# A decoder layer on one Trainium2 core: the five steps from sums to shares stand apart among the maxima

## The chip, the cores and the metric

The kernel runs on one core of one Trainium2 chip. The metric is the device time of one execution in microseconds (us). The engines are TensorE (PE in the rows; its weight loads are PEld), VectorE (DVE), ScalarE (ACT), GpSimd (POOL) and SyncE (SP), whose instruction stream issues most DMAs (SPq).

## The reference, cut to what matters

One decoder layer with normalisation ahead of each part, for x of 4 x 1024 x 256 in f32: self-attention (16 heads of 16, causal), cross-attention over 77 context rows with a mask, and a gated feed-forward part of width 768, each added to the residual. What the change touches is the softmax of both attentions:

```
scores = jnp.where(causal[None, None], scores, -jnp.inf)
attn = jax.nn.softmax(scores, axis=-1)
out = jnp.einsum('bhqk,bkhd->bqhd', attn, V).reshape(b, s, H * hd)
return out @ Wo.T + bo
...
attn = jax.nn.softmax(scores, axis=-1)
out = jnp.einsum('bhqk,bhkd->bhqd', attn, v)
```

## The kernel before, in words

The phases follow each other: projections, self-attention, a middle part (output projection, residual, normalisation, queries of the cross-attention), cross-attention, feed-forward. Every engine has its own program, and semaphores alone tie them together.

Both attentions work in 16 groups: GB = 4 groups for each of the 4 batches, HG = 4 heads and 1024 queries in each group. A batch is called b, a group g, and `b = g // GB - 1` in the code is the batch before the one that is being worked on.

Self-attention makes the scores twice. First TensorE makes them with queries on the partitions (`maxima`, lines 837 and 842), and VectorE takes the largest of each row (`item`, a reduction on line 767, one for each of 38 items of a group). The largest values are cut into two bf16 parts (`parts_of_max`, lines 777 to 782), turned by TensorE (line 832), copied to `mrow` (line 764) and sent by a DMA into two further rows of the queries (`stq`). Then TensorE makes the scores with keys on the partitions and the maximum taken away (`scores`, lines 856 and 860), ScalarE takes the exponential (line 814), and TensorE multiplies by the values (`products`, line 870), where a column of ones gives the sum of each softmax row. So in the loop of group g the maxima of group g + 1 stand among the scores and products of group g. Their order is a list, `ring`, of NMX = 40 items: 38 reductions and the two turned blocks `("t", 0)` (item 15) and `("t", 1)` (item 39). The order on TensorE is the list `plan`: nearly always one scores unit, one ring item, and now and then a pair of products of 16 matmuls each. The maxima use three banks of PSUM, so

```
need(t, s_mxe, N if N == N_AHEAD else N - 1 if N < N_AHEAD + 2 else N + 1 - NMB)
```

lets TensorE begin item N when VectorE is through with item N - 3 (NMB = 3). In `plan`, the first pair of products stands right behind item 6, the second right behind item 10, the third behind item 19, the fourth behind item 27, the fifth behind item 36.

The sums of a batch, 16 heads x 1024 queries, are gathered by DMA into `den` (128 x 128 f32); the last of them is the DMA on line 728 (self) or line 1508 (cross) of the function that stores a group's output. When the four groups of a batch are stored, `shares` (self) or `shares3` (cross) makes the shares 1/sum and cuts them into three bf16 parts: a reciprocal (lines 937, 1525), a copy to bf16 (940, 1528), a subtraction (943, 1531), a copy to bf16 (940, 1528) and a subtraction (945, 1533). Each step waits for the semaphore of the step before. Ahead of the first step VectorE waits for the stores of the four groups (`us`, `xus`). SyncE then writes the parts to DRAM (`store_shares`, `store_shares3`, which wait for all five steps) and reads them back; they are used a group or more later.

In self-attention `shares` stands on VectorE in the loop of groups 5, 9 and 13, behind all 39 items of the next group. In cross-attention a group has only 8 steps u, each with two matmuls of scores, and the maxima of group g + 2 are 8 reductions (line 1337, at most two a step, from u = 2 on), with the turned blocks on lines 1409 (TensorE) and 1328 (VectorE). `shares3` stands at u = 4 of groups 5, 9 and 13, ahead of that step's items. The shares of the last batch of each attention are made elsewhere (`mid_vector`, `ffn_vector`), all five steps in one piece.

SyncE's order in a cross group (`cross_sync`) is: load the queries of group g + 3 (`load_cross`), send the maxima of g + 1, half 1, store the output of group g - 1 (`store_sums3`, with the DMA on line 1508), in groups 5, 9 and 13 `store_shares3`, send the maxima of g + 2, half 0, then the weights and `load_shares3`.

Of the kernel before, what the change touches and what calls it, by code (L numbers as in the profile page):

```python
# [10 lines left out]
ALU = mybir.AluOpType  # L11
# [12 lines left out]
def need(eng, semaphore, count):  # L24

    if count > 0:
        eng.wait_ge(semaphore, count)


def program(nc, x, ctx_t, mask_t, Wq, bq, Wk_t, bk, Wv_t, bv, Wo_t, bo, W_cross, shift_w, gate,  # L30
# [11 lines left out]
    GB = H // HG  # L42
# [29 lines left out]
    with root:  # L72
# [5 lines left out]
        def sem(name):  # L78
            return root.enter_context(nc.semaphore(name))

        def sems(name, n):
            return [sem(f"{name}{i}") for i in range(n)]
# [565 lines left out]
        def mx_bank(N):  # L648
            return TB[N % 2] if N < N_AHEAD else MXB[N % NMB]
# [42 lines left out]
        us = sems("b_us", 2)  # L692
        NOUT = 16 * (HG + 1)
# [54 lines left out]
        def self_gpsimd(g):  # L748
# [5 lines left out]
            power2(g, 0)  # L754
            power2(g, 1)

        def self_vector(v, some):
            def item(g, n):
                kind, m = ring[n]
                N = g * NMX + n  # L760
                src = bank[mx_bank(N)]
                v.wait_ge(s_mxf, N + 1)
                if kind == "t":
                    nc.vector.tensor_copy(mrow[:, g % 2, m], src[0:32, 0:P // 2].bitcast(BF16)).then_inc(s_mxe, 1)
                    return
                half, k, r, h0, hb, _, w, _ = mx_units[m]
                nc.vector.tensor_reduce(pm[:, k, h0:h0 + hb, r],  # L767
                                        src[:, 0:hb * w].rearrange("p (h w) -> p h w", h=hb),
                                        AX, ALU.max).then_inc(s_mxe, 1)
                if m == n_half - 1 or m == len(mx_units) - 1:  # L770
                    parts_of_max(g, half, N)

            def parts_of_max(g, c, N):
                v.wait_ge(s_mxe, N + 1)
                m = pm[:, c].rearrange("p h r -> p (h r)")
                if c:
                    nc.vector.tensor_tensor(mxv[:], m, pm[:, 2].rearrange("p h r -> p (h r)"), ALU.max).then_inc(s_cmb, 1)
                    v.wait_ge(s_cmb, 3 * g + 2)
                    m = mxv[:]
                nc.vector.tensor_copy(mt[:, c, 0], m).then_inc(s_cmb, 1)  # L780
                v.wait_ge(s_cmb, 3 * g + (3 if c else 1))
                nc.vector.tensor_tensor(mt[:, c, 1], m, mt[:, c, 0], ALU.subtract).then_inc(s_mt, 1)

            if some:
                for n in some:
                    item(0, n)
                return

            for g in range(G):
                item(g, NMX - 1)  # L790
                if g + 1 < G:
                    for n in range(NMX - 1):
                        item(g + 1, n)
                b = g // GB - 1
                if b >= 0 and g % GB == 1:
                    shares(v, b)
            mid_early_vector(v)

        def self_scalar(a):
# [100 lines left out]
        s_rd = sem("c_rd")  # L900
        s_rs = sem("c_rs")
# [25 lines left out]
        def load_shares(sp, b):  # L927
            sp.wait_ge(s_rs, 16 * (b + 1))
            sp.dma_start(rd[:, b], rd3[b].rearrange("c h s -> (c h) s")).then_inc(s_rl, 16)

        def shares(v, b):

            for w in range(2):
                v.wait_ge(us[w], NOUT * 2 * (b + 1))
            need(v, s_rs, 16 * (b - 1))
            n, q = 5 * b, b % 2
            nc.vector.reciprocal(den[:, b], den[:, b]).then_inc(s_rd, 1)
            for part in range(2):
                v.wait_ge(s_rd, n + 2 * part + 1)
                nc.vector.tensor_copy(r3[:, q, part], den[:, b]).then_inc(s_rd, 1)  # L940
                v.wait_ge(s_rd, n + 2 * part + 2)
                if part == 0:
                    nc.vector.tensor_tensor(den[:, b], den[:, b], r3[:, q, 0], ALU.subtract).then_inc(s_rd, 1)
                else:
                    nc.vector.tensor_tensor(r3[:, q, 2], den[:, b], r3[:, q, 1], ALU.subtract).then_inc(s_rd, 1)

        def spread(t, c, k):

# [35 lines left out]
        def power2(g, c):  # L984
            u = c % 3
            g.wait_ge(cs_sum, NSUM * (c + 1))
            need(g, cs_xn, J * (c - 2))
            nc.gpsimd.tensor_tensor(crstd[:, u], cve[:, u], mhalf[:], ALU.pow).then_inc(cs_pow, 1)
            g.wait_ge(cs_pow, c + 1)
            nc.gpsimd.tensor_tensor(cneg[:, u], cmom[:, u, 0], crstd[:, u], ALU.mult).then_inc(cs_nm, 1)  # L990
# [16 lines left out]
        def mid_early_vector(v):  # L1007
            for c in range(2):
                for k in range(KT):
                    quotients(v, c, k)  # L1010
                sums2(v, c)
            for k in range(KT):
                quotients(v, 2, k)
# [213 lines left out]
        xus = sems("d_us", 2)  # L1227
# [94 lines left out]
        def cross_vector(v, some):  # L1322
            def item(N):
                kind, g, m = order2[N]
                src = bank[XMXB[N % NMB]]
                v.wait_ge(xs_mxf, N + 1)
                if kind == "t":
                    nc.vector.tensor_copy(xmrow[:, g % 2, m], src[0:32, 0:P // 2].bitcast(BF16)).then_inc(xs_mxe, 1)
                elif kind == "s":
                    o = sums_of(g, m)  # L1330
                    nc.vector.tensor_tensor(o, src[:], o, ALU.mult).then_inc(xs_mxe, 1)
                elif kind == "o":
                    x_ = xres[:, g, 2 * m:2 * m + 2].rearrange("p j d -> p (j d)")
                    nc.vector.tensor_tensor(x_, src[:], x_, ALU.add).then_inc(xs_mxe, 1)
                else:
                    half, r = m // 4, m % 4
                    nc.vector.tensor_reduce(xpm[:, half, :, r], src[:, 0:HG * SK].rearrange("p (h w) -> p h w", h=HG),  # L1337
                                            AX, ALU.max).then_inc(xs_mxe, 1)
                    if r == 3:
                        v.wait_ge(xs_mxe, N + 1)  # L1340
                        top = xpm[:, half].rearrange("p h r -> p (h r)")
                        nc.vector.tensor_copy(xmt[:, half, 0], top).then_inc(xs_cmb, 1)
                        v.wait_ge(xs_cmb, 2 * g + half + 1)
                        nc.vector.tensor_tensor(xmt[:, half, 1], top, xmt[:, half, 0], ALU.subtract).then_inc(xs_mt, 1)

            if some:
                for N in some:
                    item(N)
                return
            N = len(lead2)  # L1350
            for g in range(G):
                b, i = g // GB - 1, g % GB
                if g == 1:
                    v.wait_ge(s_phase, 10)
                for u, due in enumerate(steps2[g]):
                    if b >= 0 and i == 1 and u == 4:
                        shares3(v, b)
                    for _ in due:
                        item(N)
                        N += 1  # L1360
                if g == G - 3:
                    moments3(v, 0)
                if g == G - 2:
                    normalise3(v, 0)
# [110 lines left out]
        s_rd2 = sem("e_rd")  # L1475
        s_rs2 = sem("e_rs")
# [38 lines left out]
        def load_shares3(sp, b):  # L1515
            sp.wait_ge(s_rs2, 16 * (b + 1))
            sp.dma_start(rd2[:, b % 2], xrd3[b].rearrange("c h s -> (c h) s")).then_inc(s_rl2, 16)

        def shares3(v, b):

            for w in range(2):
                v.wait_ge(xus[w], NOUT * 2 * (b + 1))
            need(v, s_rs2, 16 * (b - 1))
            n, q = 5 * b, b % 2
            nc.vector.reciprocal(den2[:, q], den2[:, q]).then_inc(s_rd2, 1)
            for part in range(2):
                v.wait_ge(s_rd2, n + 2 * part + 1)
                nc.vector.tensor_copy(xr3[:, q, part], den2[:, q]).then_inc(s_rd2, 1)
                v.wait_ge(s_rd2, n + 2 * part + 2)
                if part == 0:  # L1530
                    nc.vector.tensor_tensor(den2[:, q], den2[:, q], xr3[:, q, 0], ALU.subtract).then_inc(s_rd2, 1)
                else:
                    nc.vector.tensor_tensor(xr3[:, q, 2], den2[:, q], xr3[:, q, 1], ALU.subtract).then_inc(s_rd2, 1)

        def sums_of(c, k):
            return oall2[:, c // 2 % 2, k, c % 2 * CH:(c % 2 + 1) * CH]
# [247 lines left out]
        den = sb(keep, "den", [P, B, DT])  # L1784
        r3 = sb(keep, "r3", [P, 2, 3, DT], BF16)
# [33 lines left out]
        den2 = sb(ffn_left, "den2", [P, 2, DT])  # L1819
        xr3 = sb(ffn_left, "xr3", [P, 2, 3, DT], BF16)  # L1820
# [133 lines left out]
```

## Time and profile before

| what | value |
|---|---|
| time, median of 3 runs | 1067.87 us |
| the 3 runs | 1057.42, 1067.87, 1074.19 us |
| the profiled execution, its own time | 1068.38 us |
| its span, first to last instruction | 1066.7 us |
| mean granted clock of TensorE | 0.979 of full speed |
| TensorE busy | 1025.8 us (96%) |
| VectorE busy | 722.7 us (68%) |
| ScalarE busy | 577.6 us (54%) |

The span is 1.7 us shorter than the time of the same execution; what lies around it is start and end. The profile is of one execution, and the three runs spread over 16.8 us, so a sum made from the rows is a difference inside one execution.

### The profile page before, as it was taken

To read this page: it belongs to the slowest core of one execution; us is meant where nothing else is said; L and a number is where in the kernel's file an instruction comes from. 1 tells how busy PE (TensorE), PEld (TensorE's weight loads), DVE (VectorE), ACT (ScalarE), POOL (GpSimd) and SP (SyncE) were. 2 spreads that over 40 slices of the span, in tenths; PEclk is the share of its full clock that TensorE was granted. 3 is DMA by queue.
4 is the path that set the end of the run, shared out by engine and by line. 5 is a ranking of instruction groups with operands and counts; after the bars stand their busy time and mean duration, and the time that the engine had idled before them with its cause. 6 is when DMAs were issued, how large, how long until landed. Compare 5 with 4: busy or idle time off the path is not lost.

```text
span 1066.7 us, 19077 instructions
## 1 busy us (share of the span) xinstructions
PE 1025.8 (96%) x7059; PEld 603.9 (57%) x7108; DVE 722.7 (68%) x1603; ACT 577.6 (54%) x1093; POOL 198.3 (19%) x220
## 2 busy tenths in 40 slices
PE   5999999999999999999999999899999999999998
PEld 4877344444444444444444466444544588888887
DVE  7878887787887787877785387646566365555552
ACT  4785276676766676676675667457556411111110
POOL 6655000000000000000000034101000033333331
PEclk9999699999999999999999999869999999999999
DMA  8696903444443334444400048758673100000001
GB/s 259 207 280 209 177 6 78 82 82 82 82 69 60 65 64 78 86 85 82 81 14 19 10 122 185 174 89 159 117 130 61 33 8 21 20 21 20 20 21 40
DMA packets 82202, 93.27 MB, mean 87 GB/s; under 512 B 14676, under 2 KB 75312, under 8 KB 80573
## 3 DMA queue, kind: packets, MB, share of 16 engines
q1 hardware_dynamic: 79527, 88.85, 38.3%
q10 hardware_dynamic: 2582, 3.20, 1.4%
q8 instruction: 57, 0.93, 0.4%
q14 instruction: 36, 0.29, 0.1%
HBM read 53.55 MB, written 28.80 MB: 77 GB/s over the span
## 4 chain that ended last, share of the span: by engine, by line
PE 77%; DVE 14%; ACT 3%; issue 2%; DMA 2%; SPq 1%; POOL 0%; POOLq 0%; DVEq 0%; ACTq 0%
PE bank L134 20%; PE bank L870 12%; PE bank L837 11%; PE bank L856 9%; DVE pm L767 7%; PE bank L1544 3%; PE bank L1440 3%; PE bank L1430 2%; PE bank L1432 2%; PE bank L1141 2%; PE bank L968 2%; PE bank L860 2%; PE bank L1413 2%; PE bank L842 2%; PE bank L1415 1%
## 5 line engine op out<-in xcount | busy, mean ns | idle before, releaser
L767 DVE TENSOR_REDUCE pm<-bank 128x1 f32<-128x512 f32 (+3 forms) x608 | 356.9, 654 | 86.6 <-PE bank L842 65.6
L814 ACT ACTIVATE prob<-bank 128x512 f32<-128x512 f32 (+1 forms) x608 | 317.5, 584 | 174.0 <-PE bank L860 87.9
L837 PE MATMUL bank<-stk,stq 96*128 96x512 bf16 (+3 forms) x768 | 224.4, 336 | 5.6 <-DVE pm L767 3.2
L856 PE MATMUL bank<-stq,stk 98*128 98x512 bf16 (+3 forms) x768 | 221.5, 328 | 2.7 <-ACT prob L814 0.7
L870 PE MATMUL bank<-prob,va 128*17 128x512 f32 (+3 forms) x1536 | 145.0, 496 | 2.7
L837 PEld LDWEIGHTS bank<-stk,stq 96*128 96x128 bf16 x768 | 68.3, 98 | 134.9 <-DVE pm L767 76.8
L1692 ACT ACTIVATE e_sg<-bank 128x512 f32<-128x512 f32 x48 | 28.7, 598 | 174.4 <-PE bank L134 172.3
L1379 ACT ACTIVATE xprob<-bank 80x512 f32<-80x512 f32 x128 | 73.0, 592 | 73.8 <-PE bank L1432 70.8
L753 POOL TENSOR_TENSOR xres<-xres,bo_b 128x256 f32<-128x256 f32 x32 | 23.2, 724 | 399.2 <-DVE pm L767 204.2
L856 PEld LDWEIGHTS bank<-stq,stk 98*128 98x128 bf16 x768 | 69.1, 98 | 44.7 <-ACT prob L814 9.1
L1609 POOL TENSOR_TENSOR e_ht<-e_hf,e_ht 128x512 fp32r<-128x512 f32 x48 | 62.2, 1296 | 109.9 <-DVE e_ht L1634 109.8
L870 PEld LDWEIGHTS bank<-prob,va 128*17 128x17 f32 x1536 | 40.5, 113 | 72.8 <-issue 52.8
L860 PE MATMUL bank<-tri_k,identb 128*128 128x128 bf16 (+2 forms) x334 | 79.4, 238 | 0.0
L134 PE MATMUL bank<-e_xnt,wg 128*128 128x512 f32 x288 | 74.8, 395 | 0.8 <-ACT xu L1371 0.8
L842 PE MATMUL bank<-tri_q,identb 128*128 128x128 bf16 (+1 forms) x321 | 75.4, 235 | 0.0
L134 PE MATMUL bank<-e_xnt,wu 128*128 128x512 f32 x288 | 73.2, 389 | 0.0
L1337 DVE TENSOR_REDUCE xpm<-bank 128x4 f32<-128x320 f32 x128 | 60.1, 487 | 17.6 <-PE bank L1415 14.2
L1632 DVE TENSOR_TENSOR e_hf<-bank,e_sg 128x512 f32<-128x512 f32 x48 | 33.1, 690 | 57.3 <-ACT e_sg L1692 57.3
L134 PEld LDWEIGHTS bank<-wd,e_ht 128*128 128x128 f32 x504 | 61.4, 192 | 0.5
L134 PE MATMUL bank<-wd,e_ht 128*128 128x256 f32 x504 | 61.6, 283 | 0.0
L134 PEld LDWEIGHTS bank<-e_xnt,wu 128*128 128x128 f32 x288 | 54.1, 188 | 11.4
L134 PEld LDWEIGHTS bank<-e_xnt,wg 128*128 128x128 f32 x288 | 52.7, 188 | 12.7 <-issue 2.5
(183 smaller groups left out, 1354.6 us busy)
## 6 DMA issues: line engine op xcount, KB each, us to landing
qk<-a_parts SPq DMA_DIRECT2D x32, 384.0 KB, 2.8
xq<-c_parts SPq DMA_DIRECT2D x16, 384.0 KB, 2.7
xstq<-xq SPq DMA_DIRECT2D x32, 192.0 KB, 4.2
stq<-qk SPq DMA_DIRECT2D x30, 192.0 KB, 3.9
stk<-qk SPq DMA_DIRECT2D x15, 384.0 KB, 6.4
vs<-a_vst SPq DMA_DIRECT2D x8, 544.0 KB, 3.8
oall<-u_out SPq DMA_DIRECT2D x64, 64.0 KB
xstq<-xq SPq DMA_DIRECT2D x32, 128.0 KB, 4.5
```

What stands on the lines that cost most here:

```text
L134: mm = nc.tensor.matmul(dst, a[:, i], b[:, j], start=(n == 0), stop=(n == 3 * len(terms) - 1))
L767: nc.vector.tensor_reduce(pm[:, k, h0:h0 + hb, r], src[:, 0:hb * w].rearrange("p (h w) -> p h w", h=hb), AX, ALU.max).then_inc(s_mxe, 1)
L814: nc.scalar.activation(prob[:, U % NPS, 0:hb * n], bank[STB[U % NSB]][:, 0:hb * n], ACT.Exp).then_inc(s_ex, 1)
L837: mm = nc.tensor.matmul(dst[:, h * w:(h + 1) * w], stq[i][0:R, half, h0 + h, r * P:(r + 1) * P], stk[i][0:R, h0 + h, k0:k0 + w], start=(h ...
L842: mm = nc.tensor.matmul(dst[:, 0:hb * w].rearrange("p (h w) -> p h w", h=hb)[:, :, w - P:w], identb[:], tri_q[:, 0:hb], start=False, stop= ...
L856: mm = nc.tensor.matmul(dst[:, h * n:(h + 1) * n], stk[i][0:RM, h0 + h, kt * P:(kt + 1) * P], stq[i][0:RM, half, h0 + h, q0:q0 + n], start ...
L860: mm = nc.tensor.matmul(dst[:, 0:hb * n].rearrange("p (h n) -> p h n", h=hb)[:, :, 0:P], identb[:], tri_k[:, 0:hb], start=False, stop=True ...
L870: mm = nc.tensor.matmul(bank[PVB[half]][h * VW:h * VW + VC, q0:512], va[g % NB][:, kt, :, h], prob[:, (g * NST + first + h // hb) % NPS, ( ...
L1337: nc.vector.tensor_reduce(xpm[:, half, :, r], src[:, 0:HG * SK].rearrange("p (h w) -> p h w", h=HG), AX, ALU.max).then_inc(xs_mxe, 1)
L1379: nc.scalar.activation(xprob[:, U % NPS2], bank[STB[U % NSB]][0:SK, :], ACT.Exp).then_inc(xs_ex, 1)
L1609: nc.gpsimd.tensor_tensor(ht[:, c % 2, 1, h], hf[:, h % 2], ht[:, c % 2, 0, h].bitcast(F32), ALU.subtract).then_inc(es_hl, 1)
L1632: nc.vector.tensor_tensor(hf[:, h % 2], bank[5 + 2 * (h % 2)][:], sg[:, h % 2], ALU.mult).then_inc(es_h, 1)
```

## The change

Two functions `share_step` and `share_step3` make one of the five steps each, with the same instructions and the same waits. `shares` and `shares3` call all five in a row, and are still used so for the last batch. In the loop over groups the call is gone. In self-attention the steps now follow items 6, 12, 18, 24 and 30 of the next group's ring, in groups 5, 9 and 13 as before. In cross-attention they stand at the beginning of the steps u = 1 to 5 in place of all at u = 4. The wait for the stores (`us`, `xus`) moves with the first step.

```diff
+        SHARES_AT = (6, 12, 18, 24, 30)
...
             for g in range(G):
+                b = g // GB - 1
                 item(g, NMX - 1)
                 if g + 1 < G:
                     for n in range(NMX - 1):
                         item(g + 1, n)
-                b = g // GB - 1
-                if b >= 0 and g % GB == 1:
-                    shares(v, b)
+                        if b >= 0 and g % GB == 1 and n in SHARES_AT:
+                            share_step(v, b, SHARES_AT.index(n))
             mid_early_vector(v)
...
+        def share_step(v, b, step):
+
+            q = b % 2
+            if step == 0:
+                for w in range(2):
+                    v.wait_ge(us[w], NOUT * 2 * (b + 1))
+                need(v, s_rs, 16 * (b - 1))
+                nc.vector.reciprocal(den[:, b], den[:, b]).then_inc(s_rd, 1)
+                return
+            v.wait_ge(s_rd, 5 * b + step)
+            if step in (1, 3):
+                nc.vector.tensor_copy(r3[:, q, step // 2], den[:, b]).then_inc(s_rd, 1)
+            elif step == 2:
+                nc.vector.tensor_tensor(den[:, b], den[:, b], r3[:, q, 0], ALU.subtract).then_inc(s_rd, 1)
+            else:
+                nc.vector.tensor_tensor(r3[:, q, 2], den[:, b], r3[:, q, 1], ALU.subtract).then_inc(s_rd, 1)
+
         def shares(v, b):
...
+            for step in range(5):
+                share_step(v, b, step)
...
                 for u, due in enumerate(steps2[g]):
-                    if b >= 0 and i == 1 and u == 4:
-                        shares3(v, b)
+                    if b >= 0 and i == 1 and 1 <= u <= 5:
+                        share_step3(v, b, u - 1)
```

`share_step3` is the same as `share_step` with the names of the cross-attention (`xus`, `s_rd2`, `den2`, `xr3`).

## Rows read from the trace of the kernel before

**Rows 1.** The page: granted TensorE clock in 40 slices, and the chain by engine.

```profile
PEclk9999699999999999999999999869999999999999
...
PE 77%; DVE 14%; ACT 3%; issue 2%; DMA 2%; SPq 1%; POOL 0%; POOLq 0%; DVEq 0%; ACTq 0%
```

**Rows 2.** Timeline of VectorE, self group 5: start, duration, line, and idle time before.

```profile
304.43 0.94 DVE L937 RECIPROCAL den<-den 128x128 f32<-128x128 f32 x1
305.41 0.23 DVE L940 CAST r<-den 128x128 bf16<-128x128 f32 x1
...
306.26 0.29 DVE L945 TENSOR_TENSOR r<-den,r 128x128 bf16<-128x128 f32 x1
306.47 0.20 DVE L764 COPY mrow<-bank 32x128 bf16<-32x128 bf16 x1
```

**Rows 3.** Timeline of VectorE, line 777, one a group: the beat of the self groups.

```profile
274.04 0.18 DVE L777 TENSOR_TENSOR mxv<-pm 128x16 f32<-128x16 f32 x1
...
303.92 0.17 DVE L777 TENSOR_TENSOR mxv<-pm 128x16 f32<-128x16 f32 x1
...
334.62 0.18 DVE L777 TENSOR_TENSOR mxv<-pm 128x16 f32<-128x16 f32 x1
```

**Rows 4.** Timeline of VectorE, the reductions in the loop of self group 5.

```profile
275.70 3.75 DVE L767 TENSOR_REDUCE pm<-bank 128x4 f32<-128x512 f32 x7 [0.34 <-PE bank L832]
281.28 2.48 DVE L767 TENSOR_REDUCE pm<-bank 128x1 f32<-128x512 f32 x4 [1.83 <-PE bank L842]
...
290.26 4.74 DVE L767 TENSOR_REDUCE pm<-bank 128x1 f32<-128x512 f32 x8 [1.09 <-PE bank L837]
296.30 5.08 DVE L767 TENSOR_REDUCE pm<-bank 128x1 f32<-128x384 f32 x9 [1.29 <-PE bank L842]
```

**Rows 5.** Timeline of TensorE's weight loads in the same group, two that wait for VectorE.

```profile
286.03 0.23 PEld L837 LDWEIGHTS bank<-stk,stq 96*128 96x128 bf16 x4 [0.34 <-DVE pm L767]
...
298.44 0.10 PEld L837 LDWEIGHTS bank<-stk,stq 96*128 96x128 bf16 x1 [0.19 <-DVE pm L767]
```

**Rows 6.** Timeline of VectorE, cross groups 8 to 10, line 1328: the beat of the groups.

```profile
766.33 0.21 DVE L1328 COPY xmrow<-bank 32x128 bf16<-32x128 bf16 x1 [1.13 <-PE bank L1409]
...
774.31 0.21 DVE L1328 COPY xmrow<-bank 32x128 bf16<-32x128 bf16 x1 [1.45 <-PE bank L1409]
...
783.04 0.21 DVE L1328 COPY xmrow<-bank 32x128 bf16<-32x128 bf16 x1 [1.45 <-PE bank L1409]
```

**Rows 7.** Timeline of TensorE, cross group 9.

```profile
775.19 0.30 PE L1413 MATMUL bank<-xstk,xstq 96*128 96x80 bf16 x4
...
779.16 0.22 PE L1409 MATMUL bank<-identb,xmt 128*32 128x128 bf16 x1 [0.40 <-DVE xmt L1344]
```

**Rows 8.** Timeline of SyncE's queue: last stores of a batch's sums; loads ahead of one.

```profile
728.08 0.61 SPq L1508 DMA_DIRECT2D den<-xu  x1
...
762.94 2.93 SPq L1282 DMA_DIRECT2D xstq<-xq  x6
...
771.00 0.62 SPq L1508 DMA_DIRECT2D den<-xu  x1
...
813.40 0.62 SPq L1508 DMA_DIRECT2D den<-xu  x1
```

**Rows 9.** The chain in order of time, 728 to 740 us: its first piece.

```profile
724.43 7.30 DMA xstq<-xq
```

**Rows 10.** Timeline of VectorE, cross group 5.

```profile
731.16 0.21 DVE L1328 COPY xmrow<-bank 32x128 bf16<-32x128 bf16 x1 [1.45 <-PE bank L1409]
...
733.68 0.94 DVE L1525 RECIPROCAL den<-den 128x128 f32<-128x128 f32 x1
```

**Rows 11.** Timeline of TensorE, cross group 5.

```profile
732.79 0.30 PE L1413 MATMUL bank<-xstk,xstq 96*128 96x80 bf16 x4
```

**Rows 12.** Busy time by stretch, cross group 13; last columns: DMA share, GB/s.

```profile
815.00:816.00 1.00, 1.00 (x10) 0.24 (x10) 0.22 (x2) 1.00 (x4) 0.00 (x0) 1.00 0.04 9
```

**Rows 13.** The DMAs that write and read the shares of the cross-attention, us to landing.

```profile
xrd<-xr SPq DMA_DIRECT2D x4, 96.0 KB, 1.9
```

More of the change, by code:

```diff
@@ L929, in load_shares @@
             sp.dma_start(rd[:, b], rd3[b].rearrange("c h s -> (c h) s")).then_inc(s_rl, 16)
-        def shares(v, b):
[L933 to L945, printed above, removed]
+        def share_step(v, b, step):
[13 more added lines that the diff above has]
+                nc.vector.tensor_tensor(r3[:, q, 2], den[:, b], r3[:, q, 1], ALU.subtract).then_inc(s_rd, 1)
+        def shares(v, b):
+            for step in range(5):
+                share_step(v, b, step)
         def spread(t, c, k):
@@ L1517, in load_shares3, with share_step3 @@
             sp.dma_start(rd2[:, b % 2], xrd3[b].rearrange("c h s -> (c h) s")).then_inc(s_rl2, 16)
-        def shares3(v, b):
[L1521 to L1533, printed above, removed]
+        def share_step3(v, b, step):
+            q = b % 2
+            if step == 0:
+                for w in range(2):
+                    v.wait_ge(xus[w], NOUT * 2 * (b + 1))
+                need(v, s_rs2, 16 * (b - 1))
+                nc.vector.reciprocal(den2[:, q], den2[:, q]).then_inc(s_rd2, 1)
+                return
+            v.wait_ge(s_rd2, 5 * b + step)
+            if step in (1, 3):
+                nc.vector.tensor_copy(xr3[:, q, step // 2], den2[:, q]).then_inc(s_rd2, 1)
+            elif step == 2:
+                nc.vector.tensor_tensor(den2[:, q], den2[:, q], xr3[:, q, 0], ALU.subtract).then_inc(s_rd2, 1)
+            else:
+                nc.vector.tensor_tensor(xr3[:, q, 2], den2[:, q], xr3[:, q, 1], ALU.subtract).then_inc(s_rd2, 1)
+        def shares3(v, b):
+            for step in range(5):
+                share_step3(v, b, step)
         def sums_of(c, k):
```

## The prediction

> **What bounds the kernel now.** I read the page first: TensorE is busy 96% of the span and carries 77% of the chain that ended last, VectorE 14% [rows 1]. So a change on VectorE counts only where TensorE waits for it. Then the timeline of VectorE at a block of the five steps [rows 2]: the reciprocal starts at 304.43 and the copy to `mrow` behind the block at 306.47, so one block holds VectorE for 2.04 us. What TensorE loses by that is best read from the beat of the groups, which is the same to 0.01 us wherever nothing special stands. A self group without the block takes 303.92 - 274.04 = 29.88 us, the one with it 334.62 - 303.92 = 30.70 us [rows 3]. A cross group without it takes 774.31 - 766.33 = 7.98 us, with it 783.04 - 774.31 = 8.73 us [rows 6]; there the reader sees TensorE wait 0.40 us for the cut maxima that stand behind the block [rows 7]. The price of a block today is therefore 0.82 us in self-attention and 0.75 us in cross-attention, and there are three of each: 2.46 + 2.25 = 4.71 us. The change cannot give back more than this.
>
> **What a step costs when it stands apart.** Inside the block each step waits for the one before: the reciprocal runs 0.94 us from 304.43 to 305.37, and the next step starts at 305.41, 0.04 us later. The last step starts at 306.26 and takes 0.29 us, to 306.55, but the copy behind it, which doesn't need its result, starts at 306.47, 0.08 us before that end [rows 2]. Between maxima every step is of the second kind, on both its sides. So I take duration less 0.08 us: reciprocal 0.86, the two copies 0.15 each, the two subtractions (0.29 us each) 0.21 each, in sum 1.58 us in place of 2.04.
>
> The Trainium skill, VectorE: DVE Perf Modes, section The DRAIN you can't avoid, says that the next operation waits for the pipe to empty and that a semaphore between two operations costs nothing extra. By that a step apart would cost as much as one in the block (0.27 for a copy, 0.33 for a subtraction). This speaks against the change; the 0.08 us of overlap beside the 0.04 us of gap speak against the rule here.
>
> **Self-attention, step by step.** I lay the five places on the reductions of a group without the block [rows 4].
> - Step 0 follows item 6, the last of the seven that start at 275.70. Behind them VectorE is idle for 1.83 us, while TensorE does the first pair of products. The 0.86 us of the reciprocal fit in with 0.97 us left. Cost 0; without this cover it would be 0.86. Its wait for the stores is for the output of a group that was stored a whole group (29.88 us) earlier, so nothing queues behind it.
> - Step 1 (0.15) follows item 12. From 281.28 VectorE runs without idle time until 1.09 us before 290.26, and TensorE's weight load for item 16 waits 0.34 us for a reduction there [rows 5]: VectorE sets the pace. Cost 0.15.
> - Step 2 (0.21) follows item 18. Item 19 is the last before the products, and the 1.09 us of idle time behind it [rows 4] take it. Cost 0.
> - Step 3 (0.15) follows item 24. Items 25 to 27 end 1.29 us before 296.30 [rows 4], and TensorE asks for their banks only behind the next products. Cost 0.
> - Step 4 (0.21) follows item 30, in the run of nine that starts at 296.30. The load of item 34 waits 0.19 us for item 31 [rows 5]. Cost 0.21.
>
> That is 0.36 us in place of 0.82, a gain of 0.46 a group and 1.38 in three. Bounds: nothing lost at all gives 2.46; steps 1 and 4 at the price inside the block (0.27 + 0.33 = 0.60) give 3 x 0.22 = 0.66. A cost below nothing is excluded, since instructions are only added between maxima. SyncE's writing of the shares stands a group later and waits for nothing new.
>
> **Cross-attention.** Here the wait for the stores moves too, from u = 4 to u = 1, and this is the uncertain part. At u = 1 and 2 VectorE has no maxima. It is idle for 1.45 us before the copy of the turned block [rows 6, 10], and both the reciprocal and step 1 now stand ahead of that copy. They take 0.94 + 0.04 + 0.15 = 1.13 us and fit in 1.45, if the last store has landed. What queues behind the wait is this copy and all maxima of g + 2; TensorE misses it first at the third item after it, at 775.19 in group 9 [rows 7]. So the copy (0.21 us) may start as late as about 774.9, and the store may land at 774.9 - 1.13 = 773.8 without a loss.
> - Group 9: the store is issued at 771.00. The six loads ahead of it on the same queue were issued from 762.94 to 765.87 [rows 8]. With the 7.30 us that such a load took in group 4 [rows 9] they are through at about 772.7, and a store took 1.9 us elsewhere [rows 13]: landing about 773, in time. Cost 0, gain 0.75.
> - Group 13: the rows repeat 42.4 us later (813.40 against 771.00, rows 8), so the limit is at 816.2. The DMA engines are nearly empty (share 0.04) from 815 to 816 [rows 12]. Cost 0, gain 0.75.
> - Group 5: issued at 728.08 [rows 8], while the loads ahead are through only at 724.43 + 7.30 = 731.73 [rows 9]. It lands after that, and before 733.68, when the reciprocal of today starts without idle time ahead of it [rows 10]. I take 732.4, a little below the middle. Then the copy starts at 732.4 + 1.13 = 733.53 and ends at 733.74, and TensorE, which used to start its third item at 732.79 [rows 11], stands about 1.0 us. That replaces 0.75: a loss of 0.25. With 731.7 it would be a gain of 0.5, with 733.68 a loss of 1.5.
>
> Steps 2 to 4 (0.21 + 0.15 + 0.21) stand singly between reductions where the whole block fitted with 0.75 us of loss; cost 0. Step 4 at u = 5 is later than before only by the items of u = 4, and SyncE asks for it behind the four stores of the group. Sum of the cross part: 0.75 + 0.75 - 0.25 = 1.25.
>
> The Trainium skill, DMA: Bandwidth & Descriptors, section Anatomy of one DMA, puts the fixed part of a DMA at about 2.0 us. By it alone the store of group 5 would land at 730.1.
>
> **The sum.** 1.38 + 1.25 = 2.6 us less. The profiled execution took 1068.38 us (span 1066.7 and 1.7 around it); it would become 1065.8. It stands 0.5 us above the median of the three runs, 1067.87, which would become 1065.3.
>
> **The rivals.**
> - The store of group 5 lands as fast as the write of the shares does, 1.9 us after its issue [rows 13], at 730.0. Then the copy stands at 731.13, before its 731.16, and the cross part gains 2.25: 1067.87 - 3.6 = 1064.2. Against it: the queue ahead. The fixed time in the skill's DMA page leads to the same. 15%.
> - Slower: the wait for the stores takes the place of the block. Every us of lateness beyond my landings (732.4 in group 5, the limit 773.8 in group 9) costs TensorE 1 us, and from 2.6 us in sum the kernel is slower. Group 5 can add 1.3 (to 733.68); group 9 as much as 2.8, if its store took the 5.6 us that group 5 allows (771.00 + 5.6 = 776.6). That is 4.1 in all: 1.5 us slower, 1069.4. 12%.
> - The steps land where VectorE sets the pace, all five: 1.58 us a self group in place of 0.82, a loss of 2.3, with the cross gain 1.0 slower: 1068.9. Against it: the idle 1.83 us. 5%.
> - The change does not do what it says: TensorE gets its banks sooner but waits as long for something else, such as the queries of the next groups, for which it stood in group 5 until 731.73 [rows 9]. 1067.9. 13%.
> - TensorE's clock falls elsewhere. It is granted less than full in three of 40 slices (0.6, 0.8 and 0.6) [rows 1], each 26.7 us; a slice more or less at 1.2 in place of 2.4 GHz is 6 to 13 us, and the 16.8 us between the three runs are of this size. Waits of a us in places where the clock is full do not speak for it. 10%, both ways.
> - My forecast, 1065.3: 45%.
>
> **How the numbers follow.** All cases but the clock lie between 1064.2 and 1069.4. The median of a few runs adds its own uncertainty; single runs lay 10.5 below and 6.3 above the median, and I allow 7 below and 4 above, some two thirds of that. This gives 1057 to 1073. Changes within 2% (21 us), about what a measurement of this kernel can tell from no change, hold every case but a rare one of the clock: 96% within, 2% on either side.
>
> **What would show it.** In the profile after: five single steps with no idle time ahead of the self ones; self groups with them at 30.2 us (30.0 to 30.5) against 29.88; the reciprocal in cross groups 9 and 13 just ahead of the copy on line 1328, and those groups at 7.98 us; in group 5 VectorE idle ahead of the reciprocal until about 732.4 less what self-attention gave, and TensorE idle about 1 us for the copy. Wrong I would be if the beat of self groups 5, 9 and 13 stays at 30.7, or if groups 9 and 13 wait for the store as well.

## The result, and the profile after

| | before | after |
|---|---|---|
| median | 1061.04 us | 1065.0 us |
| lowest to highest | 1057.42 to 1074.23, and one of 3491.92 | 1059.05 to 1077.07 |
| the profiled execution, its own time | 1068.38 us | 1064.74 us |
| its span, mean granted clock | 1066.7 us, 0.979 | 1063.0 us, 0.982 |

The ratio is 1.0043, with a 95% interval of 1.0022 to 1.0064, from 21 runs of each: the change makes the kernel about 4 us slower. I had forecast 2.6 us faster. The ratios leave out runs over 1.5% above the fastest of their kernel (three of before and two of after); the means below leave out only the run of 3491.92, and without the others they would be about 1 us lower for before, after and versions 1 to 3, which changes no reading. The two profiled executions alone would say the opposite, because the one of before took 7.3 us more than the median of its kernel.

To see inside 4 us I split the span of every run. Span times mean granted clock is about the time that the run would take with TensorE at full speed, "full-clock time" below; the rest of the span is "lost to low clock". (Of a stretch at 1.2 GHz half counts as lost.) Before: 1045.9 and 15.0 us (33 runs beside the first experiments; 35 beside the second gave 1045.8 and 13.4). After: 1044.3 and 20.7 us. So the kernel does need less time at full clock, by 1.6 us, and loses some 6 us more to a lower clock. These are means over runs that differ: single runs of before lost 6 to 29 us, of after 14 to 31.

VectorE in the changed kernel, timeline, self group 5 and the cross groups 5, 9 and 13 (lines are shifted: 777 is now 779, 1328 is 1335, 1409 is 1416, 1413 is 1420; the reciprocals are on 940 and 1533, the copies to bf16 on 944 and 1537):

```profile
273.59 0.18 DVE L779 TENSOR_TENSOR mxv<-pm 128x16 f32<-128x16 f32 x1
...
275.25 3.75 DVE L769 TENSOR_REDUCE pm<-bank 128x4 f32<-128x512 f32 x7 [0.34 <-PE bank L834]
278.91 0.94 DVE L940 RECIPROCAL den<-den 128x128 f32<-128x128 f32 x1
...
303.81 0.17 DVE L779 TENSOR_TENSOR mxv<-pm 128x16 f32<-128x16 f32 x1
...
333.69 0.18 DVE L779 TENSOR_TENSOR mxv<-pm 128x16 f32<-128x16 f32 x1
...
712.49 0.21 DVE L1335 COPY xmrow<-bank 32x128 bf16<-32x128 bf16 x1 [0.77 <-PE bank L1416]
...
719.49 0.95 DVE L1533 RECIPROCAL den<-den 128x128 f32<-128x128 f32 x1 [5.01 <-DMA den<-xu]
720.48 0.23 DVE L1537 CAST xr<-den 128x128 bf16<-128x128 f32 x1
720.62 0.20 DVE L1335 COPY xmrow<-bank 32x128 bf16<-32x128 bf16 x1
...
767.54 0.21 DVE L1335 COPY xmrow<-bank 32x128 bf16<-32x128 bf16 x1 [0.77 <-PE bank L1416]
...
771.64 0.95 DVE L1533 RECIPROCAL den<-den 128x128 f32<-128x128 f32 x1 [2.11 <-DMA den<-xu]
...
772.77 0.20 DVE L1335 COPY xmrow<-bank 32x128 bf16<-32x128 bf16 x1
...
776.72 0.21 DVE L1335 COPY xmrow<-bank 32x128 bf16<-32x128 bf16 x1 [0.39 <-PE bank L1416]
...
810.38 0.21 DVE L1335 COPY xmrow<-bank 32x128 bf16<-32x128 bf16 x1 [0.77 <-PE bank L1416]
...
812.56 0.95 DVE L1533 RECIPROCAL den<-den 128x128 f32<-128x128 f32 x1 [0.19 <-DMA den<-xu]
...
813.81 0.21 DVE L1335 COPY xmrow<-bank 32x128 bf16<-32x128 bf16 x1
...
818.36 0.21 DVE L1335 COPY xmrow<-bank 32x128 bf16<-32x128 bf16 x1 [0.56 <-PE bank L1416]
```

Read it against [rows 3, 6 and 10]. The reciprocal of the self group stands right behind item 6, in the idle 1.83 us, and the group takes 303.81 - 273.59 = 30.22 us in place of 30.70; the one without steps still takes 29.88. The three cross groups are three different cases. In group 13 the reciprocal waits 0.19 us, the copy stands 3.43 us behind the one before it, and the group takes 818.36 - 810.38 = 7.98 us: the block's 0.75 us are saved. In group 9 the wait for the store is 2.11 us, the copy comes 5.23 us behind the one before it, and the group takes 776.72 - 767.54 = 9.18 us, longer than with the block (8.73). In group 5 the wait is 5.01 us and the copy comes 8.13 us behind.

TensorE in cross group 5, timeline:

```profile
717.96 0.32 PE L1420 MATMUL bank<-xstk,xstq 96*128 96x80 bf16 x4 [2.10 <-DMA xstq<-xq]
...
720.88 0.45 PE L1420 MATMUL bank<-xstk,xstq 96*128 96x80 bf16 x4 [1.75 <-DVE xmrow L1335]
...
721.39 0.63 PE L1437 MATMUL bank<-xstq,xstk 98*128 98x512 bf16 x1
```

and the same kernel by stretch (busy time of the engines, then granted clock, DMA share, GB/s), with the page's row of the clock:

```profile
PEclk9999699999999999999999999996999999999999
...
710.00:720.00 10.00, 7.02 (x62) 2.82 (x58) 3.70 (x11) 6.06 (x13) 1.00 (x1) 1.00 1.12 195
720.00:730.00 10.00, 9.12 (x49) 4.04 (x50) 5.21 (x17) 3.73 (x8) 0.99 (x1) 0.50 0.36 68
730.00:740.00 10.00, 10.00 (x52) 4.37 (x51) 3.53 (x11) 4.16 (x8) 0.00 (x0) 0.50 0.61 102
740.00:750.00 10.00, 9.76 (x64) 4.37 (x63) 5.04 (x12) 4.78 (x10) 1.00 (x1) 0.98 0.54 90
```

TensorE stands twice within 5 us, 2.10 us for queries and 1.75 us for the copy behind the wait. Then the granted clock goes from 1.00 (2.4 GHz) to 0.50 (1.2 GHz) for some 20 us: a matmul of 512 columns that took 0.38 us takes 0.63. The clock is low although TensorE is busy again (10.00 of 10 us from 730 on). That stretch alone costs about 10 us, half its length; in the profile of before a low stretch lay ahead of group 5 instead, from 686 to 710 (the 0.8 and the 0.6 late in [rows 1]).

Why the stores land so differently is on SyncE's queue (timeline, issues only):

```profile
706.88 0.41 SPq L1260 DMA_DIRECT2D iw<-up_t  x1
707.33 2.85 SPq L1289 DMA_DIRECT2D xstq<-xq  x6
...
713.41 0.61 SPq L1515 DMA_DIRECT2D den<-xu  x1
...
759.15 0.41 SPq L1260 DMA_DIRECT2D iw<-down_t  x1
759.60 2.98 SPq L1289 DMA_DIRECT2D xstq<-xq  x6
...
767.67 0.61 SPq L1515 DMA_DIRECT2D den<-xu  x1
...
810.52 0.61 SPq L1515 DMA_DIRECT2D den<-xu  x1
```

and in the chain in order of time:

```profile
713.41 5.98 DMA den<-xu
```

The reciprocals start at 719.49, 771.64 and 812.56, so the same store of 16 KB takes about 6.0, 4.0 and 2.0 us. Ahead of the first two, by 6.5 and 8.5 us, stands a load of 768 KB of feed-forward weights; ahead of the third there is none.

### The profile page after: what moved, and what is told of

Its sections match the earlier page's. It is cut to its first block, busy times and chain, and to the rows that moved or that the text cites. A ratio compares the mean times of both kernels' runs of the same rounds, so it can differ in the third digit from the quotient of the medians.

```text
span 1063.0 us, 19077 instructions
## 1 busy us (share of the span) xinstructions
PE 1020.8 (96%) x7059; PEld 603.8 (57%) x7108; DVE 720.3 (68%) x1603; ACT 576.4 (54%) x1093; POOL 198.5 (19%) x220
## 4 chain that ended last, share of the span: by engine, by line
PE 78%; DVE 13%; ACT 3%; issue 2%; DMA 2%; SPq 1%; POOL 0%; POOLq 0%; DVEq 0%; ACTq 0%
PE bank L134 20%; PE bank L872 12%; PE bank L839 11%; PE bank L858 9%; DVE pm L769 7%; PE bank L1556 3%; PE bank L1447 3%; PE bank L1437 2%; PE bank L1439 2%; PE bank L1148 2%; PE bank L975 2%; PE bank L862 2%; PE bank L1420 2%; PE bank L844 2%; PE bank L1422 1%
```

## The experiments

Each version was timed in 10 to 12 runs, beside runs of the kernel before. By the spread of the runs a mean in the column "full clock" is uncertain by 0.2 to 0.4 us (one standard error of the mean), one in the column "lost" by 0.7 to 1.9 us.

| version | median | ratio, 95% | full clock | lost |
|---|---|---|---|---|
| before | 1060.78 to 1061.65 | | 1045.8 to 1046.2 | 13.4 to 15.0 |
| after | 1065.0 | 1.0043 [1.0022, 1.0064] | 1044.3 | 20.7 |
| 1 self part only | 1060.79 | 1.0001 [0.9972, 1.0029] | 1044.3 | 16.2 |
| 2 cross part only | 1068.76 | 1.0067 [1.0032, 1.0101] | 1046.4 | 21.0 |
| 3 wait only | 1063.12 | 1.0006 [0.9974, 1.0038] | 1046.8 | 15.4 |
| 4 cross steps later | 1055.21 | 0.9943 [0.9923, 0.9964] | 1042.2 | 11.3 |
| 5 group 5 alone later | 1057.4 | 0.9958 [0.993, 0.9986] | 1043.2 | 11.6 |
| 6 first two steps only | 1066.53 | 1.0055 [1.0027, 1.0083] | 1045.7 | 18.9 |
| 7 steps later, and a stand | 1065.86 | 1.0061 [1.0034, 1.0088] | 1043.5 | 20.9 |
| 8 as 4, self places moved | 1054.82 | 0.9946 [0.9921, 0.9971] | 1040.2 | 13.0 |
| 9 after, both loads early | 1055.14 | 0.9952 [0.993, 0.9973] | 1041.1 | 12.3 |
| 10 before, both loads early | 1057.63 | 0.9965 [0.9941, 0.9988] | 1045.0 | 10.9 |
| 11 as 8, both loads early | 1055.2 | 0.9948 [0.9927, 0.9969] | 1040.3 | 12.4 |
| 12 after, one load early | 1056.79 | 0.9949 [0.9925, 0.9973] | 1042.3 | 12.2 |

**1. The self part only.** The changed kernel with the cross-attention's five steps in one piece again.

```diff
-                    if b >= 0 and i == 1 and 1 <= u <= 5:
-                        share_step3(v, b, u - 1)
+                    if b >= 0 and i == 1 and u == 4:
+                        shares3(v, b)
```

> Only the self-attention part of the change; the cross-attention has its five steps in one piece at u = 4 as before. Theory A (the wait for the stores, moved from u = 4 to u = 1 in the cross-attention, makes TensorE stand, and its clock is then low for some 20 us): the self groups 5, 9 and 13 take 30.2 us in place of 30.7, 1.4 us faster than before (ratio 0.9987), and what the change lost is gone. Theory B (the change itself loses nothing; the low clock in the cross-attention comes as often without it): also about 1.4 us faster, and no other variant differs from it by more than 2 us. Theory C (something in the self part loses the time): 3 to 5 us slower than before (ratio 1.003 to 1.005).

The full-clock time falls by 1.6 us, so the self part is worth what was forecast (1.38). The median doesn't show it: 16.2 us are lost to low clock, with an uncertainty of 1.6, no fewer than before. Its cross-attention is that of before, and in its profile the block at u = 4 of group 5 waits 1.08 us for the store; TensorE then stands 2.07 us for the cut maxima behind the block, and 10 us at 1.2 GHz follow. So the kernel before is not free of this wait either.

**2. The cross part only.**

```diff
-                        if b >= 0 and g % GB == 1 and n in SHARES_AT:
-                            share_step(v, b, SHARES_AT.index(n))
+                if b >= 0 and g % GB == 1:
+                    shares(v, b)
```

> Only the cross-attention part of the change; the self-attention has its five steps in one piece. Theory A: 5 to 7 us slower than before (ratio 1.005 to 1.007), VectorE stands over 2 us ahead of the reciprocal in cross group 5, and the granted clock is 1.2 GHz for about 20 us after that, unless it was low just before. Theory B: within 2 us of before. Theory C: within 2 us of before.

The loss is all in the cross part: 0.5 us of full-clock time and 6.0 us of low clock, ratio 1.0067. Its group 5 shows the same pair of stands (TensorE's timeline), though in this one execution only 3.4 us at 1.2 GHz follow them, and 6.8 us lie ahead, between 680 and 700:

```profile
724.03 0.32 PE L1420 MATMUL bank<-xstk,xstq 96*128 96x80 bf16 x4 [1.14 <-DMA xstq<-xq]
...
727.37 0.32 PE L1420 MATMUL bank<-xstk,xstq 96*128 96x80 bf16 x4 [2.17 <-DVE xmrow L1335]
```

**3. The wait only.** The kernel before, with one more wait for the stores at u = 1; the block stays at u = 4.

```diff
+                    if b >= 0 and i == 1 and u == 1:
+                        for w in range(2):
+                            v.wait_ge(xus[w], NOUT * 2 * (b + 1))
                     if b >= 0 and i == 1 and u == 4:
                         shares3(v, b)
```

> The kernel before, with nothing but the wait for the stores (xus) put at u = 1 of cross groups 5, 9 and 13; all five steps stay in one piece at u = 4. Theory A: the wait alone does it, 5 to 8 us slower than before (ratio 1.005 to 1.0075), a little more than with the cross part of the change, since the block still costs 0.75 us a group. Theory B and C: within 2 us of before. If only the steps and not the wait were at fault, this one would be as fast as before.

VectorE waits as long (5.43 us), but nothing stands between the landing and the copy, and TensorE's second stand is 0.69 us:

```profile
721.54 0.21 DVE L1328 COPY xmrow<-bank 32x128 bf16<-32x128 bf16 x1 [5.43 <-DMA den<-xu]
```

```profile
719.96 0.32 PE L1416 MATMUL bank<-xstk,xstq 96*128 96x80 bf16 x4 [2.46 <-DMA xstq<-xq]
...
721.81 0.45 PE L1416 MATMUL bank<-xstk,xstq 96*128 96x80 bf16 x4 [0.69 <-DVE xmrow L1328]
```

Full-clock time rises by 0.9 us. The profiled execution has a low stretch of 17 us here, but over 12 runs 15.4 us are lost (uncertain by 1.9), against 15.0 before: the 5 to 8 us that I expected from the wait alone did not come, and the ratio allows 4 us at most. It seems to take the reciprocal and the copy to bf16 behind the wait (1.1 us) as well; version 6 tests that.

**4. The cross steps later.** The five steps stand at u = 4, 5, 6, 7 and behind the last item of the group, apart as in the change.

```diff
-                    if b >= 0 and i == 1 and 1 <= u <= 5:
-                        share_step3(v, b, u - 1)
+                    if b >= 0 and i == 1 and u >= 4:
+                        share_step3(v, b, u - 4)
...
+                if b >= 0 and i == 1:
+                    share_step3(v, b, 4)
```

> The self part as in the change; in the cross-attention the steps stand apart too, but from where the block was: the reciprocal with its wait at u = 4, the next at u = 5, 6, 7, and the last behind the items of u = 7. Theory A: no standing for the stores, cross groups 5, 9 and 13 lose 0 to 0.2 us in place of 0.75, and the kernel is about 3.6 us faster than before (ratio 0.9966). Theory B: 1.5 to 3.6 us faster too, but then the other variants don't differ from it by more than those steps. Theory C: slower than before like the change.

```profile
717.22 0.21 DVE L1335 COPY xmrow<-bank 32x128 bf16<-32x128 bf16 x1 [1.45 <-PE bank L1418]
...
721.07 0.94 DVE L1535 RECIPROCAL den<-den 128x128 f32<-128x128 f32 x1
...
727.28 0.21 DVE L1335 COPY xmrow<-bank 32x128 bf16<-32x128 bf16 x1 [0.74 <-PE bank L1418]
```

The reciprocal starts without idle time ahead of it. The group takes 727.28 - 717.22 = 10.06 us, 7.98 and TensorE's 2.0 for queries, with the clock full. Full-clock time is 3.7 us below before, 3.7 us less are lost to low clock, and the ratio is 0.9943. I had expected 3.6 us in all; it is 6, since the clock gives back as much again. Taking the block apart pays; its place at u = 1 does not, with the weights loaded where they are.

**5. Group 5 alone later.** As in 4, but for b = 0 only; groups 9 and 13 keep the change's places.

> The change, but in cross group 5 alone the steps stand late (the reciprocal with its wait at u = 4, then u = 5, 6, 7 and the end), while groups 9 and 13 keep u = 1 to 5. Theory A (the wait at u = 1 of group 5 makes TensorE stand and that brings the low clock): nearly all of the loss is gone. Time at full clock (span times granted clock) falls from 1044.3 to about 1042.7, the time lost to the low clock from 20.7 to 11 to 14 us, the whole to about 1056 us (ratio 0.995 to 0.997), with group 9 still at about 9.2 us in place of 8.0. Rival D (the losses come from all three groups alike): about 1060 to 1063 us, low clock still 17 us or more.

11.6 us are lost in place of 20.7, and the ratio falls from 1.0043 to 0.9958. Group 9 still waits (its reciprocal at 759.90 behind 2.46 us), which goes with 1.0 us more of full-clock time than in version 4 and no clock (11.6 against 11.3 us lost, each uncertain by 0.8). So the loss of clock comes from group 5, as far as 12 runs can tell. At u = 4 of group 5 the reciprocal waits 0.76 us for the store here, without a stand of TensorE.

**6. The first two steps only.** The kernel before with steps 0 and 1 at u = 1 and 2, the other three in one piece at u = 4.

> The self-attention as before; in the cross-attention the first two steps with the wait stand at u = 1 and 2, the other three in one piece at u = 4. Theory A: the copy of the turned block comes as late as with the change (the landing and 1.1 us for the two steps), so the low clock costs about as much as with the cross part of the change (21 us, against 15 before and 15.4 with the wait alone), and the ratio is 1.004 to 1.008. Rival E (the wait alone cost nothing in the median by chance, the two steps add no more than their 1.1 us): 1.000 to 1.002, low clock 15 us.

Against version 3 this adds the two steps behind the wait. They bring TensorE's second stand from 0.69 to 2.25 us and the loss to 18.9 us. That is clearly more than before (13.4), but only 3.5 us above version 3, and that difference is uncertain by 2.1: that the steps matter beside the wait is likely and not proven.

**7. A stand without the wait.** Version 4, whose profile shows no wait for the store, with about 6 us of idle work added on VectorE at u = 1 of group 5: a memset and two reciprocals of a buffer that nothing reads there.

```diff
+                    if g == 5 and u == 1:
+                        nc.vector.memset(exn[:, 0, 0:2], 1.0).then_inc(s_dum, 1)
+                        for n in range(2):
+                            v.wait_ge(s_dum, n + 1)
+                            f = exn[:, 0, 0:2].rearrange("p j d -> p (j d)")[:, 0:400]
+                            nc.vector.reciprocal(f, f).then_inc(s_dum, 1)
+                        v.wait_ge(s_dum, 3)
```

> The version with late steps, and at u = 1 of cross group 5 some 6 us of work on VectorE that nothing needs (a fill and two reciprocals on scratch), so that TensorE stands there without any wait for a store. Theory A: TensorE stands 3 to 5 us in group 5 in place of 2.0, time at full clock 1042.2 + 2 to 3 = 1044 to 1045, and the time lost to the low clock rises from 11 to 17 to 22 us, as with the change: 1062 to 1067 us in all (ratio 1.001 to 1.006). Rival F (it is the DMAs under way or the order of the steps and not the standing that lowers the clock): only the 2 to 3 us are added, low clock stays at 11 to 12 us, 1056 to 1058 us.

```profile
721.13 5.34 DVE L1369 RECIPROCAL e_xn<-e_xn 128x400 f32<-128x400 f32 x2
726.50 0.21 DVE L1336 COPY xmrow<-bank 32x128 bf16<-32x128 bf16 x1
```

```profile
723.28 0.32 PE L1430 MATMUL bank<-xstk,xstq 96*128 96x80 bf16 x4 [1.34 <-DMA xstq<-xq]
...
726.77 0.45 PE L1430 MATMUL bank<-xstk,xstq 96*128 96x80 bf16 x4 [1.83 <-DVE xmrow L1336]
```

A late copy alone, with another cause, brings the same pair of stands and the same loss: 20.9 us in place of 11.3, while full-clock time rises by 1.3. So it is the late copy, and TensorE's stand behind it, that brings the loss, whatever makes the copy late. (In this one execution about 7 us at 1.2 GHz fall in group 5, from 724 on, and about 10 us between 680 and 700, as in other versions.)

**8. Other places in self-attention.** Version 4, with the five self steps behind items 6, 6, 19, 27 and 36, where products of TensorE follow.

> The version with late steps in the cross-attention, and in the self-attention the steps where VectorE is idle anyway: two behind item 6, then one behind items 19, 27 and 36. The working of the prediction (a step costs its duration less 0.08 us where VectorE sets the pace, nothing ahead of idle time) says self groups 5, 9 and 13 at 29.9 us in place of 30.2, 1.0 us less than the version with late steps in all (ratio to before 0.993). If a step costs nothing in either place, no difference; if items 19, 27 and 36 are not covered, 30.2 to 30.5 us a group.

The self groups with steps take as long (303.80 - 273.91 = 29.89) as those without: the remaining 0.34 us a group are gone. Full-clock time falls by 2.0 us more (uncertain by 0.6), of which these rows explain 1.0. With 13.0 us lost the median is only 0.4 us below version 4, so the two can't be told apart by the time.

**9. The changed kernel, weights early.** Only two loads of weights move on SyncE's queue, from its groups 3 and 7 to 1 and 6. VectorE's and TensorE's programs are those of the change.

```diff
-                if g in (0, 3, 7):
-                    load_weight(sp, (0, 3, 7).index(g))
+                if g in (0, 1, 6):
+                    load_weight(sp, (0, 1, 6).index(g))
```

> The changed kernel with one more edit: the two later loads of feed-forward weights (768 KB each, on SyncE's queue) stand in SyncE's groups 1 and 6 in place of 3 and 7. Theory A: the store that ends a batch lands late (5.98 us behind its issue in group 5, 3.97 in group 9, against 2.04 in group 13) because such a load was put on the queue 6.5 and 8.5 us before it. Then it lands about 2 to 3 us behind its issue in both groups, the copy of the turned block stands 3.43 us behind the start of the group as in group 13, the groups take about 8.0 us, TensorE doesn't stand in group 5, and full-clock time falls from 1044.3 to about 1042 (or 2 us more if the wait for the queries of 2.1 us only moves to group 2 or 3); lost to low clock 11 to 14 us; median about 1056. Rival B: the store is slow because of the loads of queries (768 KB a group) that stand ahead in every group: the landings stay at 4 to 6 us, the time near 1065.

SyncE's issues of the two stores, and VectorE in groups 5 and 9:

```profile
719.92 1.03 SPq L1515 DMA_DIRECT2D den<-xu  x1
...
761.58 0.61 SPq L1515 DMA_DIRECT2D den<-xu  x1
```

```profile
719.80 0.21 DVE L1335 COPY xmrow<-bank 32x128 bf16<-32x128 bf16 x1 [0.77 <-PE bank L1416]
...
722.71 0.95 DVE L1533 RECIPROCAL den<-den 128x128 f32<-128x128 f32 x1 [0.93 <-DMA den<-xu]
...
727.79 0.21 DVE L1335 COPY xmrow<-bank 32x128 bf16<-32x128 bf16 x1 [0.39 <-PE bank L1416]
...
761.45 0.21 DVE L1335 COPY xmrow<-bank 32x128 bf16<-32x128 bf16 x1 [0.77 <-PE bank L1416]
...
763.62 0.95 DVE L1533 RECIPROCAL den<-den 128x128 f32<-128x128 f32 x1 [0.19 <-DMA den<-xu]
```

The stores now take 2.8 and 2.0 us, group 5 takes 727.79 - 719.80 = 7.99 us, and the version is 10 us faster than the change: ratio 0.9952 in place of 1.0043. TensorE has no stand over 0.6 us in group 5 any more, for the copy or for queries, so version 10 is needed to say how much the loads give by themselves.

**10. The kernel before, weights early.** The same edit on the kernel before.

> The kernel before, with both weight loads moved (SyncE's groups 1 and 6). Its shares don't wait for the store, so Theory A gives it only what TensorE loses to the queries in group 5 (0.7 to 2.1 us), and that may come back in group 2 or 3: full-clock time 1044 to 1046, median 1058 to 1062. If it gains as much as the changed kernel does, the weights matter by themselves and not through the store.

The loads matter a little by themselves: 1.1 us of full-clock time and 3.1 us less lost than in the runs beside it (14.0). But against this version the changed steps (version 9) gain 1045.0 - 1041.1 = 3.9 us of full-clock time, about what my first rival priced them at (3.6). The medians differ by less, 1057.63 - 1055.14 = 2.5 us. The median of version 10 lies just below the 1058 to 1062 that I expected.

**11. Both together.** Version 8 with the loads early.

> The best version so far (shares from u = 4 on, self steps behind items 6, 6, 19, 27, 36) with both weight loads moved. Theory A: the stores already landed in time, so only TensorE's wait for queries in group 5 can go: full-clock 1039 to 1040.5, median 1052 to 1055. Against the run with the changed kernel and both loads moved it should be equal to within 1 to 3 us of full-clock time: where the store lands in time, u = 1 is as good as u = 4 and only the self places differ.

Equal to 8 (1040.3 against 1040.2), and 0.8 us of full-clock time from version 9: where the store lands in time, u = 1 is nearly as good as u = 4, for the self places of version 8 alone are worth 1.0 us by their rows.

**12. One load early.** The changed kernel with only the load of SyncE's group 3 in group 1; the other stays in group 7.

> The changed kernel with only the second weight load moved, from SyncE's group 3 to 1; the third stays in group 7, so each of the two groups is a control for the other. Theory A: group 5 as in the run with both moved (landing 2 to 3 us behind the issue, no stand of TensorE, 8.0 us), group 9 as in the changed kernel (landing about 4 us, beat about 9.2 us); full-clock time 1042.3, that is 1.2 us above the run with both moved (1041.1); lost to low clock 11 to 14 us; median about 1056. Rival B: the gain of the run with both moved came from somewhere else than the store: group 9 changes too, or group 5 doesn't.

```profile
718.89 0.21 DVE L1335 COPY xmrow<-bank 32x128 bf16<-32x128 bf16 x1 [0.77 <-PE bank L1416]
...
721.89 0.95 DVE L1533 RECIPROCAL den<-den 128x128 f32<-128x128 f32 x1 [1.01 <-DMA den<-xu]
...
726.96 0.21 DVE L1335 COPY xmrow<-bank 32x128 bf16<-32x128 bf16 x1 [0.39 <-PE bank L1416]
...
760.63 0.21 DVE L1335 COPY xmrow<-bank 32x128 bf16<-32x128 bf16 x1 [0.77 <-PE bank L1416]
...
764.77 0.95 DVE L1533 RECIPROCAL den<-den 128x128 f32<-128x128 f32 x1 [2.15 <-DMA den<-xu]
...
769.84 0.21 DVE L1335 COPY xmrow<-bank 32x128 bf16<-32x128 bf16 x1 [0.39 <-PE bank L1416]
```

Group 5 is mended (8.07 us) and group 9 is as in the change (9.21 us, wait 2.15), in one and the same run. Full-clock time is 1.2 us above version 9, as expected. So each store is late because of the weight load ahead of it. All profiles agree: with the load in its old place the store of group 5 lands 5.3 to 6.3 us behind its issue and that of group 9 3.4 to 4.3 us (ten and eleven profiles, by their records of semaphore updates); with the load moved it is 1.9 to 3.1 us and 2.0 us.

## Why the prediction was wrong

**What held.** The beat of the self groups: 30.22 us against 30.2 forecast, three times, and 1.6 us of full-clock time against 1.38. Duration less 0.08 us as the price of a step apart held too: the copy to `xmrow` starts at 720.62, 0.09 us before the step ahead of it ends (720.48 + 0.23 = 720.71). Group 13 gained its 0.75. The Trainium skill, VectorE: DVE Perf Modes, section The DRAIN you can't avoid, spoke against the change with its rule that the next operation waits for the pipe to empty. The same page's section Two Vector instructions with no wait between them only holds an instruction back in certain cases, so that others start before the one ahead has finished; the 0.09 us agree with that, though the copy has a wait of its own here, for TensorE, which was over long before.

**The step that failed: the landing of the stores.** Group 5: I took 732.4, which is 4.3 us behind the issue; it is 6.0. Group 9: I took 773, 2 us behind, against a limit of 773.8; it is 4.0, past the limit by 1.2 us. Most of this stood in the trace of before. Its record of semaphore updates, which I had not read, has the last update of the two stores at 733.43 and 774.36, so 1.0 and 1.4 us later than I took, and group 9 past its limit. I let the store land 0.7 and 0.3 us behind the loads of queries (731.73 and 772.7); in that record it lands 1.7 us behind them both times. The rest is that before's execution had landings at the short end: 5.35 and 3.36 us behind the issues, where the other profiles with the loads in place have 5.3 to 6.3 and 3.5 to 4.3. Whether its low clock from 686 to 710, ahead of the weight load, has to do with that is not shown. And I looked at the loads of queries right ahead of the store, not at the weights ahead of these, though they stand in SyncE's order. With the landings as measured the rows give for the cross part: group 13 gains 0.75, group 9 loses 9.18 - 8.73 = 0.45, group 5 has 1.75 us of TensorE's waiting in place of 0.75 and loses 1.0. That is a loss of 0.7 where I had a gain of 1.25; version 2 measured 0.5. This term takes the forecast down from 2.6 to about 0.7 us of gain, and 1.6 us were measured at full clock: it made the gain smaller, but did not turn it into a loss.

**The step that turned the sign: the clock, which the sum put at nothing.** I had it as a rival at 10%, with 6 to 13 us, and without a place. "Waits of a us in places where the clock is full do not speak for it" was wrong. By the sum at full clock the change would still be 1.6 us faster; the result is slower because TensorE's stands in group 5, which the late store brings about, add 5.7 to 7.3 us of low clock on average. The trace of before had a case of it (TensorE's timeline): a stand of 2.07 us for the maxima of another group, and from 686 to 710 the clock was at 1.2 GHz.

```profile
685.35 0.39 PE L1430 MATMUL bank<-xstq,xstk 98*128 98x512 bf16 x1 [2.07 <-DMA xstq<-xmrow]
```

Versions whose profile has a stand of 1.75 us or more for the copy in group 5 (after, 2, 6 and 7) lose 18.9 to 21.0 us, those without such a one (4, 5, 8 to 12) 10.9 to 13.0, and before and version 3 lie between, at 13.4 to 15.4. Even the slower rival, which named the mechanism (the wait takes the place of the block), had a price at full clock and could reach only 1.5 us.

**The first rival**, that the store lands in time and the change gives 3.6 us, is what versions 4 and 9 measured: 3.7 us of full-clock time with the steps later, 3.9 with the weights out of the way.

**What was luck.** The time that I forecast, 1065.3 us, is nearly the 1065.0 that were measured. It was reached from the wrong start: the three runs that I had of before gave 1067.87, the 21 give 1061.04. A start 6.8 us too high and a change of -2.6 in place of +4.0 cancel.

**What stays open.** One profiled execution can't say how often the clock falls in group 5; the losses are means over 10 to 35 runs. The profiles don't give one rule. After a pair of stands in group 5 the clock was at 1.2 GHz for 20.5 us (after), 17 us (versions 3 and 6), 7 us (version 7) and 3.4 us (version 2). A single stand of 2.07 us was followed by 24 us of it in before and by 10 us in version 1, one of 2.02 us in version 4 by none. Version 3 stood 2.46 and 0.69 us, and lost no more than before on average; version 1 lies between the two sorts with 16.2 us. That late copies raise the loss on average is shown; what exactly makes the clock fall in one run and not in another is not settled. Half of the 2.0 us of version 8 is unexplained.

## What to carry to other kernels

When a step with a wait for a DMA is moved forward, read the landing of that DMA from what the queue holds ahead of it, one and two groups back (a load of 768 KB 6.5 and 8.5 us earlier made a 16 KB store take 6.0 and 4.0 us in place of 2.0). Where the trace holds the landing itself, read it there, and in more than one execution. Work that waits belongs behind the work that others need: here the same five steps at u = 4 gained 3.7 us of full-clock time and 6 us in all. And where TensorE bounds the kernel, a stand of two us can cost more than two us; compare the granted clock over many runs, not in one profile.

## What the runs showed of the hardware that I had not expected

Two stands of TensorE of 2.1 and 1.75 us, 1.2 us of work apart, were followed by some 20 us at 1.2 GHz, with TensorE busy in nearly all of them (9.12 and 10.00 of 10 us); in other profiles stands of this size were followed by 24, 17, 10, 7, 3.4 or 0 us of it. A DMA of 16 KB took 2.0, 2.8, 4.0 or 6.0 us by what stood ahead of it on the same queue. The Trainium skill, DMA: Bandwidth & Descriptors, section Anatomy of one DMA, gives about 2.0 us as the fixed part, fitted there to DMAs that GpSimd issues. The store of group 13, on SyncE's queue, agrees with 2.04 us; groups 5 and 9 took 6.0 and 4.0 behind the weights.
